# Joint attention: the context's two pairs of maximum tiles stand between a head's own pairs, not behind the last of them

## The reference, cut to what matters

```
def _L0_xattn_ref(x, context, Wq, bq, Wks, bks, Wvs, bvs, Wkc, bkc, Wvc, bvc, Wo, bo):
    q = x @ Wq + bq
    k = jnp.concatenate([x @ Wks + bks, context @ Wkc + bkc], axis=1)
    v = jnp.concatenate([x @ Wvs + bvs, context @ Wvc + bvc], axis=1)
    ...
    attn = jnp.einsum('bhqd,bhkd->bhqk', q, k) / jnp.sqrt(jnp.float32(head_dim))
    attn = jax.nn.softmax(attn, axis=-1)
    out = jnp.einsum('bhqk,bhkd->bhqd', attn, v)
```

## Time and profile before

| | us |
|---|---|
| median of 3 runs | 2709.77 |
| lowest, highest | 2703.93, 2713.39 |
| the profiled execution's own time | 2706.77 |
| its span, first to last instruction | 2705.0 |
| the loop of the joint attention in it | about 86 to 526 of the span |

### The profile page before, as it was taken

One profiled execution on the slowest core, in us unless ns is written; L12 is line 12 of the kernel. 1 busy time (PEld: TensorE's weight loads), 2 busy tenths in 40 slices (PEclk: granted clock), 3 DMA queues, 4 the chain that ended last, 5 costly groups with the idle time before them and its releaser, 6 DMA issues. The chain is left out here.

```text
span 2705.0 us, 43103 instructions
## 1 busy us (share of the span) xinstructions
PE 2249.9 (83%) x15530; PEld 1605.4 (59%) x15536; DVE 1813.3 (67%) x3908; ACT 1380.9 (51%) x3183; POOL 1070.4 (40%) x1121
## 2 busy tenths in 40 slices
PE   6899999979987999779999877877897887885254
PEld 5344344457765666558777656767776766773122
DVE  6888888556655555566565567676658676557796
ACT  4588888634434544333333224655434655323697
POOL 1322232024434433145555245453435463432554
PEclk9799999879998999889999898999898988897586
DMA  4344444010001000020000010001000000001000
GB/s 101 37 50 48 49 50 48 10 73 1 1 9 57 1 1 1 16 106 1 1 1 1 28 53 1 2 1 54 35 1 1 1 1 36 1 1 55 0 1 32
DMA packets 13457, 65.31 MB, mean 24 GB/s; under 512 B 4928, under 2 KB 5440, under 8 KB 11584
## 3 DMA queue, kind: packets, MB, share of 16 engines
q0 software_dynamic: 8064, 18.19, 5.8%
q1 hardware_dynamic: 5184, 44.38, 4.7%
HBM read 39.41 MB, written 2.10 MB: 15 GB/s over the span
## 5 line engine op out<-in xcount | busy, mean ns | idle before, releaser
L2706 ACT ACTIVATE probs<-psum 128x512 f32<-128x512 f32 (+1 forms) x640 | 344.3, 601 | 110.2 <-PE psum L2643 93.7
L2745 DVE TENSOR_REDUCE max_parts<-psum 128x1 f32<-128x512 f32 x512 | 314.4, 674 | 47.8 <-PE psum L2591 47.7
L194 PE MATMUL psum<-x_upper,weights_upper 128*128 128x512 f32 (+2 forms) x624 | 255.9, 410 | 38.9 <-POOL weights_rest L206 24.7
L194 PE MATMUL psum<-x_rest,weights_upper 128*128 128x512 f32 (+2 forms) x624 | 253.1, 406 | 0.0
L194 PE MATMUL psum<-x_upper,weights_rest 128*128 128x512 f32 (+2 forms) x624 | 250.5, 401 | 0.0
L2643 PE MATMUL psum<-q_stack,k_stack 50*128 50x512 f32 (+1 forms) x640 | 244.0, 464 | 0.3 <-ACT probs L2706 0.3
L206 POOL TENSOR_TENSOR weights_rest<-L1f,weights_upper 128x256 fp32r<-128x256 f32 x216 | 177.1, 848 | 167.7 <-ACT weights_upper L334 167.7
L194 PE MATMUL psum<-weights_upper,hidden_upper 128*128 128x256 f32 (+2 forms) x768 | 233.1, 303 | 3.0 <-DVE x_tok L387 1.7
L194 PE MATMUL psum<-weights_upper,hidden_rest 128*128 128x256 f32 (+2 forms) x768 | 217.8, 284 | 0.0
L194 PE MATMUL psum<-weights_rest,hidden_upper 128*128 128x256 f32 (+2 forms) x768 | 217.8, 284 | 0.0
L2653 PE MATMUL psum<-probs,v_tok 128*17 128x256 f32 (+1 forms) x2560 | 203.9, 402 | 0.2 <-ACT probs L2706 0.2
(11 more groups left out here) (473 smaller groups left out, 6070.1 us busy)
## 6 DMA issues: line engine op xcount, KB each, us to landing
k_stack<-k_parts POOLq DMA_DIRECT2D x56, 147.2 KB, 3.8
L1f<-in_L1f SPq DMA_DIRECT2D x1, 7936.0 KB, 21.4
L0f<-in_L0f SPq DMA_DIRECT2D x1, 4744.0 KB, 14.9
L2f<-in_L2f SPq DMA_DIRECT2D x2, 2268.0 KB, 8.8
L1x<-in_L1x SPq DMA_DIRECT2D x1, 4226.0 KB, 12.9
k_stack<-k_parts POOLq DMA_DIRECT2D x56, 73.6 KB, 4.1
L2a<-in_L2a SPq DMA_DIRECT2D x2, 2048.0 KB, 11.3
q_stack<-q_parts POOLq DMA_DIRECT2D x56, 64.0 KB, 3.3
```

The costliest lines, as they stand in the source:

```text
L194: ins = pe.matmul(out, lhsT(a).bitcast(F32R), rhs(b).bitcast(F32R), start=start and n == 0, stop=stop and n == len(PASSES) - 1, skip_group ...
L2706: act.activation(pb[0:m, n % NPB, (1 - e) * 512:(2 - e) * 512], net.ps[0:m, ST + (2 * n + e) % NS, :], ACT.Exp, scale=HD ** -0.5)\
L2745: ins = v.tensor_reduce(mx3[:, u % 2, a + 4 * e, k:k + 1], src, AX.X, ALU.max)
```

## The change

The list `pairs` gets a new order: own pairs 0 and 1, the context's first pair, own pairs 2 and 3, the context's second, own pairs 4 to 7. Counted from 0 the context's pairs now stand at places 2 and 5 of ten, before at 8 and 9. Everything else (number and size of all products and reductions, banks, the ring's length, semaphores) is as before; ring, waits and `finish_max` follow the list.

```
-            pairs = [("self", j, k) for j in range(4) for k in range(2)] + [("ctx", i, 0) for i in range(2)]
+            own = [("self", j, k) for j in range(4) for k in range(2)]
+            pairs = own[0:2] + [("ctx", 0, 0)] + own[2:4] + [("ctx", 1, 0)] + own[4:8]
             NPAIR = len(pairs)
```

## The result

| | before | changed |
|---|---|---|
| median, us | 2704.68 (7 runs) | 2689.77 (7 runs) |
| lowest to highest, us | 2700.54 to 2713.39 | 2683.85 to 2697.90 |
| ratio, 95% interval | | 0.994, 0.9921 to 0.9960 |

What follows compares the result with a forecast made beforehand. PE was taken to bound the kernel, with ACT pacing step 1. From 2709.77 us, falls -13.3, pace -1.2 and start -0.4 gave 2694.9, stated as 2695; own range 2689 to 2701, whole range to 2712.

Steps and rivals of the forecast that it cites:

- The mechanism of the clock: Just behind step 1 of some heads: PE's weak work there lowers the clock; 512-column matmuls there remove all nine falls.
- the start: Ahead of the first scores: four of DVE's twelve reductions become short, worth -0.4 us, bounds 0 and -0.8.
- the pace: PE's time per head: -0.10 in step 1, +0.06 in steps 3 and 4, by 30 heads -1.2 us.
- only the last round may gain: Step 1's fourth round: 0.44 us with a context tile, about 0.34 with an own one, -0.10 per head.
- nine falls: Loop's drops to 1.2 GHz, each costing a head 1.48 us: all taken as gone, -13.3 us, bounds 0 and -13.3.
- the long stretch: Steps 2, 3, 4 and 0 of a head: PE sets the pace, a half step taking 1.22 us.
- stall of 0.75 us: Step 1, before the fourth round: PE has little work while ACT sets the pace; falls follow behind it.
- The rule weighed in the prediction: Falling clock needs idle gaps several times step 1's stall; falls would come back elsewhere, leaving -1.6 us alone.
- The falls stay: Step 1's stall and two narrow products lower the clock, not the short tiles: nine falls remain, 2708 us, chance 0.20.
- Some stay: Only the weaker of the hit heads still fall, some four of nine: 2701 us, chance 0.13.
- The slower one: Short rounds in steps 3 and 4 cost 0.44 each, not 0.34: +9.0 us, 2718 with falls in place, chance 0.07.
- +0.03 a half step: Cost of context tiles in step 3's first half and step 4's second half, +0.06 us a head.

Runs made afterwards that it cites:

- wide_ctx: Kernel before, order kept, with the context's maximum matmuls widened from 154 to 256 columns: ratio 0.9968 to the kernel before.
- short_own: Changed kernel with step 1's own tiles cut to two matmuls of 154 columns, DVE reducing 308 elements: ratio 0.9991 to the kernel before.
- after_again: The changed kernel run once more, nothing altered: ratio 0.9956 to the kernel before.
- places_6_7_again: Repeat of the kernel with both context pairs in step 0, otherwise like the changed kernel: ratio 0.9954 to the kernel before.
- places_6_7: Changed kernel with both context pairs at places 6 and 7 (step 0) instead: ratio 0.9937 to the kernel before.
- one_moved: Kernel before with only one context pair moved, to place 2, the other left at the last place: ratio 1.0002 to the kernel before.

## Why the prediction was right or wrong, point by point

**Which steps failed.** The mechanism of the clock held. Three other terms did not. The first is what the sum was counted from: "The median of the three runs stands 3.0 above that execution, so 2709.77 - 14.9". Seven runs of the kernel before have their median at 2704.68, 5.1 lower, and this is the distance between the forecast 2695 and the measured 2689.77. The second is the start, put at -0.4 with bounds 0 and -0.8: the first scores came 0.16 us later and the first copy 3.1 us earlier, and the latter by chance. The third is the pace, "only the last round may gain": it gained nothing. The terms beside the profiled pair, whose spans differ by 17.1 us:

| term | forecast, us | measured in the profiled pair, us |
|---|---|---|
| nine falls | -13.3 | -13.1 |
| pace | -1.2 | -2.3 |
| start | -0.4 | -3.1 |
| last head, apart from the ninth fall | 0 | -1.5 |
| rest of the kernel | 0 | +2.9 |

That the gain between the medians is 14.9, as forecast, is in part luck: the last four terms are off by 1 to 3 us each, and in the second comparison the gain was 12.

**What bounds a head.** Right. PE paces the long stretch, and ACT the third and fourth round of step 1; the wait before the fourth is the same after the change. The "stall of 0.75 us" is the time from the third start to the fourth; PE itself was idle for 0.27 of it.

**The clock.** Right in sign, place and size. The step read "I take all nine as gone: -13.3", and -13.1 was measured. Of the nine, eight lay between the first and the thirtieth copy. There the loop lost 13.9 us, of which 29 x 0.08 = 2.3 is pace, so 11.6 for eight falls, 1.45 each. The ninth gave 1.46 more (the head from the thirtieth copy took 13.42 before and 11.96 after):

```profile
501.18 0.38 ACT L2688 COPY o_heads<-psum 128x256 f32<-128x256 f32 x1
...
514.60 0.38 ACT L2688 COPY o_heads<-psum 128x256 f32<-128x256 f32 x1
```

```profile
484.19 0.38 ACT L2689 COPY o_heads<-psum 128x256 f32<-128x256 f32 x1
...
496.15 0.38 ACT L2689 COPY o_heads<-psum 128x256 f32<-128x256 f32 x1
```

What was argued from position alone is shown now: wide_ctx takes the falls away without moving anything, short_own brings five back with everything moved. It isn't absolute: after_again and places_6_7_again had one fall each. The rule weighed in the prediction (the Trainium skill, "TensorE: Matmul & The Clock Gate", section "Why this matters for your kernels", idle gaps of TensorE) doesn't explain these falls. In the view of the waits over the loop of before PE's longest is 0.4 us and that of its weight loads 0.8 us, and filling columns into running matmuls removed the falls.

**The rivals.** "The falls stay" is out: the wait before the fourth round and the two narrow products are there as before, and the falls are gone. "Some stay" is out as a forecast for the whole; one now and then is what is left of it. The slower one is out: short rounds where PE has no slack cost less than own ones, not 0.10 more.

**Pace.** The sum was -0.04 per head and is -0.08 (13.18 to 13.10), but both of its terms were wrong, the first in size and the second in sign. The step "only the last round may gain ... -0.10" failed: that round takes 0.44 with either content. The 0.44 isn't the price of two short matmuls but that of a round which starts after a wait. So "+0.03 a half step" was built on a wrong reading: in the stretch where PE is fed ahead the short pairs give -0.01 to -0.02 in step 3 and -0.05 to -0.06 in step 4, where the scores have 26 keys. The second half of step 4 of before, from 293.04 to 294.26:

```profile
293.04 0.49 PE L2591 MATMUL psum<-k_stack,q_stack 48*128 48x512 f32 x1
...
294.26 0.50 PE L2591 MATMUL psum<-k_stack,q_stack 48*128 48x512 f32 x1
```

That is 1.22, now 1.17. The saving isn't tied to the 26 keys alone: with the context's pairs in step 0 (places_6_7) the heads were 0.05 shorter as well. What else gives it wasn't looked for.

**The start.** The term "-0.4, bounds 0 and -0.8" failed, and its bounds with it. The first scores didn't come sooner: 87.06, before 86.90. Rows of the changed kernel's start (DVE, PE, ACT):

```profile
81.68 2.48 DVE L2746 TENSOR_REDUCE max_parts<-psum 128x1 f32<-128x512 f32 x4
...
87.06 0.78 PE L2644 MATMUL psum<-q_stack,k_stack 50*128 50x512 f32 x1
...
103.53 0.38 ACT L2689 COPY o_heads<-psum 128x256 f32<-128x256 f32 x1
```

The row of DVE is the first reduction of head 1, at 81.68, before 81.29: head 0's own maximum came 0.4 us later, because at the low clock DVE waited for PE behind the short tiles, 0.17 us twice. The second of these waits:

```profile
75.33 4.87 DVE L2746 TENSOR_REDUCE max_parts<-psum 128x1 f32<-128x512 f32 x8 [0.17 <-PE psum L2592]
```

What made the profile 3.1 us earlier at the first copy is the clock, back at 1.00 from 93:

```profile
83.00:92.50 9.50, 8.24 (x40) 4.58 (x44) 9.33 (x18) 4.35 (x8) 0.00 (x0) 0.50 0.01 2
93.00:98.00 5.00, 5.00 (x59) 2.11 (x51) 4.46 (x11) 3.55 (x7) 0.00 (x0) 1.00 0.00 0
```

and in the kernel before still low up to 99:

```profile
93.00:99.00 6.00, 6.00 (x37) 1.90 (x29) 3.07 (x7) 2.17 (x4) 0.00 (x0) 0.50 0.00 0
```

Above I showed this to be chance. The prediction left out that the time at which the clock returns can move; it returns at one of several, up to 24 us apart.

**DVE.** Right: 0.05 us of cover was forecast for `finish_max`, 0.14 was left, and nobody waited. Counted from the start of step 2 `finish_max` comes 0.67 later (0.46 ahead of it before, 0.21 behind it now), near the 0.76 of the sum.

**The size and the range.** Forecast -14.9. Measured -14.9 by the medians and -16 by the ratio in the first comparison, and -12 in the second. The clock and the pace explain 15.4 of the 17.1 us between the profiled executions; in the second pair of profiles the loop alone differs by 11.3, with one fall against nine. The first copy and the last head moved by 1.5 to 6.8 us between two executions of one kernel, without any change: the last head took 11.98 and 10.48 in the two of before, 10.46 and 11.96 in the two of the changed kernel. The "two or three microseconds for the rest" were too little for this. That 2689.77 lies at the low edge of the forecast's own range of 2689 to 2701 comes from the base; counted from 2704.68 the same range is 2684 to 2696, with the result in its middle.

**What stays open.** Whether the wait in step 1 or the two narrow products must come on top of the short tiles for a fall wasn't tried. That six falls of one_moved ended at 363 isn't explained, nor why short_own had five falls and not eight, nor what sets how long the low clock lasts at the start, nor the 2.9 us of the rest of the kernel.

## What to carry to other kernels

Read the granted clock head by head, not as a mean: a loop with most heads equal and every third or fourth longer by the same amount shows a clock that falls in one place of the body. In this kernel the small matmuls didn't belong in the step where PE waits; the full-size ones cost nothing there, and the small ones cost nothing where the engine never stops. That is worth a try elsewhere; that the wait is a condition wasn't shown. Before a term is read from one round or one start, see whether it began after a wait, and whether it comes again in a second execution. And count a forecast from a base that has as many runs as the result will have: three runs stood 5.1 us above seven.

## What the runs showed of the hardware that was not expected

- The clock fell to 1.2 GHz while PE was busy nearly all the time. It needed no long idle stretch: PE's longest wait in the loop was 0.4 us. With 256 columns in place of 154 in step 1's maximum matmuls, at the same pace and with the same waits, no fall came in 404 us.
- At the start of the stage the low clock lasted from 23.9 to 47.8 us in executions of nearly the same program, 44.4 in one and 23.9 in the other of the same kernel; for 27.5 us of the 44.4 PE had hardly a gap (27.48 busy).
- Two rounds of short context matmuls cost as much or a little less than two of long ones (1.17 and 1.21 against 1.22 us for a half step), with 512-column scores running beside either in other rows.
